# A two-layer gated cross-attention block: layer 0 also stores its turned context to DRAM, and layer 1 loads it in place of a turn by DMA

## The reference, cut to what matters

```python
def reference(x, ctx_1024, ...):          # x: 16 x 56 x 128, ctx_1024: 16 x 1500 x 128
    x = x + tanh(g_xattn[0]) * L0_xattn(ctx_1024, ctx_1024, layernorm(x), mask, ...)  # 16 heads of 8
    x = x + tanh(g_ffn[0])   * L0_ffn(layernorm(x), ...)       # top-1 of 8 experts + a shared one
    x = x + tanh(g_xattn[1]) * L1_xattn(layernorm(x), ctx_1024, ...)                  # 16 heads of 64
    x = x + tanh(g_ffn[1])   * L1_ffn(layernorm(x), ...)       # ternary weights, 8-bit activations
    return x
```

## Time and profile before

| | |
|---|---|
| median of 3 runs | 1309.55 us (1305.81 to 1319.06) |
| profiled execution | 1312.12 us, of which the span is 1310.4 us |
| TensorE (PE) busy | 1144.0 us, 87% |
| VectorE (DVE) busy | 892.8 us, 68% |
| ScalarE (ACT) busy | 698.3 us, 53% |
| GpSimd (POOL) busy | 510.6 us, 39% |
| DMA queue of SP | 147.11 MB, 54.8% of 16 engines |
| HBM | 61.93 MB read, 12.80 MB written |

### The profile page before, as it was taken

How to read it: one execution, slowest core, us unless ns; L and a number is a source line. 1 busy time by engine, 2 the same in 40 slices (tenths; PEclk the granted TensorE clock), 3 DMA queues, 4 the chain that set the end, 5 groups by cost and what they waited for, 6 DMA issues and landing times.

```text
span 1310.4 us, 27967 instructions
## 1 busy us (share of the span) xinstructions
PE 1144.0 (87%) x10056; PEld 654.3 (50%) x10056; DVE 892.8 (68%) x1250; ACT 698.3 (53%) x967; POOL 510.6 (39%) x344
## 2 busy tenths in 40 slices
PE   0769899999999998777879889899999989899974
PEld 0335556665665656533434455454555545455542
DVE  6456666666666673687777667677576857767668
ACT  0435455555555555445666546466465656556542
POOL 5157766666765633234022222323232322222220
PEclk9979899999999999699999999899999999999996
DMA  5144344443444353003029987989688888988530
GB/s 158 50 127 138 109 123 125 135 137 121 127 135 139 115 126 80 6 2 47 1 55 155 142 145 142 153 141 154 130 159 144 148 152 147 155 147 151 106 69 15
DMA packets 271256, 151.00 MB, mean 115 GB/s; under 512 B 233713, under 2 KB 244449, under 8 KB 271201
## 3 DMA queue, kind: packets, MB, share of 16 engines
q1 hardware_dynamic: 264944, 147.11, 54.8%
q10 hardware_dynamic: 6256, 3.16, 1.0%
HBM read 61.93 MB, written 12.80 MB: 57 GB/s over the span
## 4 chain that ended last, share of the span: by engine, by line
PE 62%; DVE 12%; issue 8%; ACT 6%; DMA 5%; SPq 3%; ACTq 3%; POOL 0%; DVEq 0%; POOLq 0%
PE bank L853 11%; PE bank L871 11%; PE bank L728 7%; PE bank L752 6%; PE bank L756 5%; PE bank L769 4%; PE bank L821 4%; DMA region<-wg_sb 3%; ACTq L385 3%; DVE neg_max L1546 2%; DMA region<-u_w 2%; DVE region L1696 2%; SPq L462 2%; DVE e_row L1507 2%; PE bank L829 2%
## 5 line engine op out<-in xcount | busy, mean ns | idle before, releaser
L1507 DVE CUSTOM_DVE_ANT_0 e_row<-bank,region 112x1500 f32<-112x1500 f32 x128 | 220.1, 1720 | 125.4 <-PE bank L728 124.0
L1201 ACT ACTIVATE region<-bank 125x896 f32<-125x896 f32 x192 | 176.0, 917 | 202.6 <-PE bank L756 202.6
L1546 DVE TENSOR_REDUCE neg_max<-bank 128x1 f32<-128x1500 f32 x112 | 192.5, 1719 | 126.5 <-PE bank L853 126.3
L853 PE MATMUL bank<-region 128*128 128x500 f16 x1008 | 234.5, 378 | 3.2 <-ACT e_row L1228 1.8
L1237 ACT COPY region<-bank 128x768 f16<-128x768 f16 x224 | 177.9, 794 | 108.0 <-PE bank L821 108.0
L1228 ACT ACTIVATE e_row<-bank,neg_shift 128x1500 f32<-128x1500 f32 x112 | 169.2, 1511 | 81.8 <-DVE neg_shift L1550 41.8
L554 POOL CAST u_w<-e_row 128x1500 f16<-128x1500 f32 x56 | 80.6, 1440 | 242.1 <-ACT e_row L1228 214.3
L554 POOL CAST wg_sb<-e_row 128x1500 f16<-128x1500 f32 x56 | 83.1, 1484 | 211.6 <-ACT e_row L1228 147.5
L853 PEld LDWEIGHTS bank<-region 128*128 (+1 forms) x1008 | 97.3, 98 | 108.3 <-issue 4.0
L752 PE MATMUL bank<-row_of,region 112*128 112x448 bf16 x384 | 137.7, 359 | 7.9 <-ACT region L1201 7.9
L871 PE MATMUL bank<-region 125*128 125x384 f16 (+1 forms) x576 | 130.8, 359 | 14.5 <-DMA region<-wg_sb 12.0
(11 more groups left out here) (218 smaller groups left out, 1524.4 us busy)
## 6 DMA issues: line engine op xcount, KB each, us to landing
region<-region SPq DMA_DIRECT2D x192, 96.0 KB, 2.2
region<-split_rows SPq DMA_DIRECT2D x72, 250.0 KB
c_in<-in_ctx SPq DMA_DIRECT2D x16, 750.0 KB
split_rows<-region SPq DMA_DIRECT2D x16, 750.0 KB
region<-in_mask_Bx1xSxS_if SPq DMA_DIRECT2D x32, 328.1 KB
g_w<-split_rows SPq DMA_DIRECT2D x24, 250.0 KB
x_norm_t<-inverse_rows SPq DMA_DIRECT2D x16, 256.0 KB, 4.6
x_norm_t<-inverse_rows SPq DMA_DIRECT2D x16, 192.0 KB, 6.6
```

The source lines that it names most:

```text
L853: last = pe.matmul(score_banks1(par, t)[:, k, :], q1[:, ql, b, 128 * t:128 * (t + 1)], c_t1[par][:, 4 * k:4 * k + 4, cl, 0:KP], start=(ql ...
L1201: act.activation(p0[:, 2 * i:2 * i + 2, :], ring0("s", h, i)[0:KP, :, 0:HALF_ROWS], ACT.Exp, scale=SCALE0)\
L1507: dve.tensor_tensor_reduce(out=masked.rearrange("p (a k) -> p a k", a=3), in0=bank[0:R0, 0:3, 0:4 * KP], in1=mask_bias[par][:].rearrange(" ...
L1546: dve.tensor_reduce(neg_max[:, t:t + 1], score_banks1(par, t), AX.XY, ALU.max, negate=True)\
```

## The change

Layer 0 gets one more transfer per batch: behind the stacking copies SP stores `c_t0` whole, 768 KB, to a DRAM tensor `turned_rows[b]` of the same layout. ScalarE waits for the store of the batch before ahead of its next copy into `c_t0`. Layer 1 no longer loads `split_rows` for a turn and no longer turns the context by DMA: at t = 1 and t = 3 of a batch SP loads the high and the low half of `turned_rows[b + 1]`, 384 KB each, straight into the next batch's `c_t1`, whose layout is now [feature, n, c, p] instead of [feature, c, n, p]. TensorE's scores wait for these loads where they waited for the turn. The buffer `c_split1` is left unused in its place. `split_rows` and the loads into `c_keep1` stay.

```diff
--- before.py
+++ after.py
@@ -221,11 +221,11 @@
         out1_w = carve([128, H, 128])
         assert queries_dead <= (B - 3) * ROWS // 2 and scores_dead <= hole_at
         assert at[0] == split_at
-        c_split1 = carve([128, KC, 2, E], F16)
+        carve([128, KC, 2, E], F16)
         c_keep1 = [carve([128, KC, 2, E], F16)[0:KP],
                    g_w[:].rearrange("p e i -> p (e i)")[0:KP, 0:KC * E].bitcast(F16)
                    .rearrange("p (c n e) -> p c n e", c=KC, n=2)]
-        c_t1 = [carve([128, KC, 2, 128], F16) for _ in range(2)]
+        c_t1 = [carve([128, 2, KC, 128], F16) for _ in range(2)]
         GROUPS1 = [(0, 4), (4, T1)]
         before_p1 = at[0]
         p1 = [carve([128, 2, KC, 128 * (b - a)], F16) for a, b in GROUPS1]
@@ -260,6 +260,7 @@
 
         inverse_row = place[0:4].rearrange("p g d -> p (g d)")
         split_rows = nc.dram_tensor("split_rows", [B, KP, KC, 2, E], F16, kind="Internal").ap()
+        turned_rows = nc.dram_tensor("turned_rows", [B, 128, 2, KC, 128], F16, kind="Internal").ap()
         inverse_rows = nc.dram_tensor("inverse_rows", [2, ROWS], F32, kind="Internal").ap()
 
         bank = ctx.enter_context(nc.psum_tensor("bank", [128, 8, 512], F32))
@@ -410,12 +411,16 @@
             wait_apart(sp, "sp", (sem("low0"), b + 1))
             sp.dma_start(split_rows[b], c_split0[0:KP].rearrange("p c n g d -> p c n (g d)")).then_inc(sem("split_out0"), 16)
 
-        def sync_split_in(sp, b, third):
-
-            if third == 0:
-                wait_apart(sp, "sp", (sem("c_turned1"), 16 * b))
-            part = slice(4 * third, 4 * third + 4)
-            sp.dma_start(c_split1[0:KP, part], split_rows[b, :, part]).then_inc(sem("split_in1"), 16)
+        def sync_turned_out(sp, b):
+
+            wait_apart(sp, "sp", (sem("ct_done0_1"), b + 1))
+            sp.dma_start(turned_rows[b], c_t0).then_inc(sem("turned_out0"), 16)
+
+        def sync_turned_in(sp, b, par, n):
+
+            if n == 0:
+                wait_apart(sp, "sp", (sem("scores1"), (b - 1) * T1))
+            sp.dma_start(c_t1[par][:, n], turned_rows[b, :, n]).then_inc(sem("turned_in1"), 16)
 
         def sync_keep(sp, b, par, third):
 
@@ -454,13 +459,6 @@
             sp.dma_start(x_norm_t[:, 128 * a:128 * z],
                          inverse_rows[par, 128 * a:128 * z].unsqueeze(0).broadcast_to((128, 128 * (z - a))))\
                 .then_inc(sem("inverse1"), 16)
-
-        def sync_turn_context1(sp, b, par):
-
-            wait_apart(sp, "sp", (sem("split_in1"), 48 * (b + 1)))
-            wait_apart(sp, "sp", (sem("scores1"), (b - 1) * T1))
-            sp.dma_start_transpose(c_t1[par].rearrange("p c n k -> p (c n) k"), c_split1.rearrange("p c n e -> p (c n e)"))\
-                .then_inc(sem("c_turned1"), 16)
 
         @block.sync
         def _(sp):
@@ -489,33 +487,30 @@
                     if not (isinstance(b, int) and b + 2 >= B):
                         sync_load_context(sp, b + 2, par)
                     sync_stack(sp, b + 1, 1 - par)
+                    sync_turned_out(sp, b + 1)
                     if not (isinstance(b, int) and b + 2 >= B):
                         sync_load_mask(sp, b + 2)
             sync_split_out(sp, 0)
             sync_stack(sp, 0, 0)
+            sync_turned_out(sp, 0)
             sync_load_mask(sp, 1)
             batches(sp, layer0)
 
             sp.wait_ge(sem("split_out0"), 16 * B)
-            sp.wait_ge(sem("ct_turned0"), 2 * B)
-            for third in range(3):
-                sync_split_in(sp, 0, third)
+            sp.wait_ge(sem("turned_out0"), 16 * B)
             sp.wait_ge(sem("st0"), B * 2 * NP)
             load(sp, "in_down0", [
                 (d_w[:, 0:NE].rearrange("p e c h -> p (e c) h"), rt_down.rearrange("e (c p) h -> p (e c) h", p=128)),
                 (d_w[:, NE], sh_down.rearrange("(c p) h -> p c h", p=128))])
 
-            sync_turn_context1(sp, 0, 0)
-            for third in range(3):
-                sync_split_in(sp, 1, third)
+            for n in range(2):
+                sync_turned_in(sp, 0, 0, n)
             sp.wait_ge(sem("w_tern"), 3)
             for third in range(2):
                 sync_keep(sp, 0, 0, third)
 
             def layer1(b, par, first, last):
                 sync_keep(sp, b, par, 2)
-                if not last:
-                    sync_turn_context1(sp, b + 1, 1 - par)
                 for t in range(T1):
                     sync_turn1(sp, b, par, t)
                     if t == 1 and not first:
@@ -526,8 +521,8 @@
                         sync_inverse_out1(sp, b, par, 0)
                     if t == 5:
                         sync_inverse_back1(sp, b, par, 0)
-                    if 1 <= t < 4 and not (isinstance(b, int) and b + 2 >= B):
-                        sync_split_in(sp, b + 2, t - 1)
+                    if t in (1, 3) and not last:
+                        sync_turned_in(sp, b + 1, 1 - par, t // 2)
                     if t >= 5 and not last:
                         sync_keep(sp, b + 1, 1 - par, t - 5)
             batches(sp, layer1)
@@ -846,12 +841,12 @@
 
         def pe_scores1(pe, b, par, t):
             if t == 0:
-                pe.wait_ge(sem("c_turned1"), 16 * (b + 1))
+                pe.wait_ge(sem("turned_in1"), 32 * (b + 1))
             wait(pe, sem("exp_done1"), b * T1 + t - 1)
             for k in range(3):
                 for ql, cl in ((0, 0), (0, 1), (1, 0)):
                     last = pe.matmul(score_banks1(par, t)[:, k, :], q1[:, ql, b, 128 * t:128 * (t + 1)],
-                                     c_t1[par][:, 4 * k:4 * k + 4, cl, 0:KP],
+                                     c_t1[par][:, cl, 4 * k:4 * k + 4, 0:KP],
                                      start=(ql == 0 and cl == 0), stop=(ql == 1))
             last.then_inc(sem("scores1"), 1)
 
@@ -1248,6 +1243,7 @@
 
             act.wait_ge(sem("ct_turned0"), 2 * b + n + 1)
             if not (isinstance(b, int) and b == 0):
+                act.wait_ge(sem("turned_out0"), 16 * b)
                 for g in range(G):
                     act.wait_ge(sem(f"stack{1 - par}_{g}"), per_use(b - 1, 1 - par, 48))
             act.copy(c_t0[:, n].rearrange("p c k -> p (c k)"),
```

## The result

The changed kernel takes 1270.44 us (median of 4 runs, 1268.9 to 1271.89) against 1308.74 us for the kernel before (4 runs, 1305.81 to 1319.06): a ratio of 0.9697, 95% interval 0.965 to 0.9744. Its profiled execution took 1269.61 us with a span of 1267.3.

The account below looks back on a forecast made before the run. TensorE was taken to bound both attentions, with only layer 1 leaving gain, in waits from SP's queue. Waits of 13.1 and 19.2 us plus 9.3 us of clock made 41.6 us off 1309.55: 1267.9, with 1 us left over 1269, range 1259 to 1296.

Parts of the forecast that it names:

- part 1: Layer 1: dropping turn L462 ends TensorE's waits at L845 (13.1 us), L871 (19.2 us) and clock losses (9.3 us): 41.6 us.
- The clock's 9.3 us: Layer 1, after 700 us: TensorE work lost to lowered clock after waits, five stretches, one of 2.5 and four of 1.7 us.
- rival C: Layer 1: second load late, L853 waits; 1 us late per batch 1284, 3 us late 1339; in full, with D, 0.07.
- The check by pairs: Layer 1: two batches of 72.94 us without L871 stall, less 1.82 idle and 1.7 clock, give 69.4 us per pair.
- The last even batch as a trial by itself: Layer 1: with turn L462 but no split_in, L845 still waits 2.13 us and L871 doesn't wait.
- part 2: Layer 1 loads: two narrow loads ahead of tile 3 cost 3.9 us at 129 GB/s, one wide 1.8 us at 215.
- part 3: Layer 1: second load behind tile 3's turn reaches the next batch's first score product with 1.2 to 2.4 us slack.
- part 4: Layer 0: the store flows 3.6 us, cost 0, or 24 us if the next context load's delay isn't taken up.
- A: Layer 1: the forecast case, all waits of both sorts go; 1262 to 1280 us, chance 0.60.
- D: Layer 0: delayed context load isn't taken up, 1293 us, or 1329 with a 6.0 us store; in full, with C, 0.07.
- E: Layer 1: nothing happens, TensorE's waits are VectorE's and ScalarE's; 1300 to 1310 us, 0.13 with mixes within 1%.
- B: Layer 1: only SP's issue time mattered, DMA engines stay full, L871's stalls remain; 1293 us, 0.20 with mild C or D.

Follow-up runs that it names:

- run 11: Changed kernel with both loads of the turned rows at the head of the batch instead of behind tiles 1 and 3: 1276.75 us, ratio 0.9731.
- run 2: Kernel before without layer 1's split-context loads at t = 1 to 3, turn by DMA kept: 1287.24 us, ratio 0.9813.
- run 3: Kernel before with the turn by DMA left out after the first two batches, loads kept: 1270.94 us, ratio 0.9676.
- run 12: Kernel before with the context's turn issued as two turns of six chunks at its old place, the batch's head: 1311.06 us, ratio 0.9999.
- runs 5: Kernel before with the turn in two halves behind tiles 1 and 3, its loads at t = 5, 6 and the next head; no store: 1309.46 us, ratio 1.0006.
- run 4: Kernel before with stored split rows padded from 125 to 128 partitions and the loads for the turn made with 128: 1288.72 us, ratio 0.9817.
- run 10: Kernel before with the turn in halves behind tiles 1 and 3, loads moved later, all split-row transfers on 128 partitions, no store: 1266.72 us, ratio 0.9656.
- run 6: Changed kernel with its second load issued behind tile 4's turn instead of tile 3's: 1317.53 us, ratio 1.0059.
- run 1: Kernel before plus only layer 0's store of the turned halves and ScalarE's wait on it: 1310.21 us, ratio 0.9983.
- run 7: Changed kernel storing the turned halves three times per batch, to three tensors, in layer 0: 1288.18 us, ratio 0.9844.
- Runs 9: Kernel before with the turn in halves behind tiles 1 and 3 and no split-context loads after batch 1: 1270.65 us, ratio 0.9686.
- run 8: Changed kernel with split rows padded to 128 partitions, for the split store and kept-context loads: 1268.08 us, ratio 0.9696.

## Why the prediction was right

**The sum (part 1).** Forecast 41.6 us, and 1269 us with one left over. Measured 38.3 us between the medians, 42.5 between the profiled executions, 41.2 in layer 1's stage. By its terms: L845's 13.1 us, gone; L871's 19.2 us, gone. The clock's 9.3 us can be held against TensorE's busy time for the same 3773 products of layer 1, before and after:

```profile
663.00:1277.00 614.00, 562.07 (x3773) 310.43 (x3774) 432.30 (x521) 359.59 (x493) 166.84 (x114) 0.98 0.80 138
662.00:1234.00 572.00, 553.18 (x3773) 306.48 (x3772) 427.42 (x514) 358.41 (x492) 165.59 (x114) 0.99 0.65 131
```

That is 8.9 us less, of 9.3 forecast, and the clock is 1.00 in each stretch from 700 to 1200 us. One premise was too general: a wait of 1.8 us doesn't always lower the clock. The kernel before waits 1.82 us at 1060.38 as at 987.44, but the clock is 1.00 from 1060 to 1066 and 0.66 from 987 to 992; and run 11, with waits of up to 1.9 us, has 1.00 over 700 to 1200. The sum counted only stretches whose fall it had seen, so it came out right; rival C's price of 1.7 us for each late load rests on the general form. The check by pairs gave 69.4 us for a pair without waits; measured 69.42. Nothing was late next: TensorE stands at 99.5 of 100 us.

**Two causes.** The last even batch as a trial by itself gave the right reading: run 2 lost L871's stalls and kept L845's wait (forecast 1284, measured 1287), run 3 lost nearly all of both (1270, 1271). The prediction said that the issue time of L462 makes the first wait, and for the kernel before that holds: tile 0's turn is issued late there (2.1 us at 824.07, and 2.8 us at 976.68, ahead of the wait of the earlier trace rows; 2.9 us in run 12) and lands in its usual 3.8 us. But it is one of two means. In runs 5 and 11 the turn is issued in time, within 0.3 us of the product that it waits for, and lands late, after 8.8 and 5.3 us. What both have in common is work in the queue ahead of tile 0's turn, and the change takes it away. One sign missed: tile 0's turn was to go out within 1 us of its low half, and goes out 3.4 us behind it (805.70, 809.12), since the prediction overlooked that it also waits for the product with V. In the sum this made no difference. With the turn landing at 812.9 and VectorE's next low half in that place at 813.15, the margin in the changed kernel is 0.2 us, which is why run 11's 1.5 us more of landing shows at once.

**The loads (part 2).** Narrow transfers at 129 GB/s against 215 was the right reading, and too small in its effect: run 4 won 24 us where I expected 14, run 10 against run 5 some 46 us by the ratios. In the changed kernel the store and the mask load behind it reach 0.98 of the engines and 300 GB/s, and the split store after them, with its 125 partitions, 0.32 and 132:

```profile
426.00:428.00 2.00, 2.00 (x39) 1.20 (x38) 1.67 (x2) 0.88 (x2) 1.92 (x2) 1.00 0.32 132
...
446.00:448.00 2.00, 2.00 (x40) 1.20 (x38) 1.85 (x2) 0.45 (x2) 0.64 (x1) 1.00 0.98 300
```

By the rule of the Trainium skill's "DMA: Bandwidth & Descriptors" ("Why a DMA increments its semaphore by 16 and not by 1") 125 partitions use 5 of 16 engines, 0.31, and 128 use all; the trace agrees. That a narrow load delays a turn on all 16 engines, by filling 5 of them, fits all these runs, but which engines are busy the profile's rows don't show.

**The second load's place (part 3).** Forecast slack 1.2 to 2.4 us; run 6 shows 3.1: the term was too careful, since the load lands in 3.6 us from its issue and isn't added whole to the turn ahead. That the place is a tight one is right: one tile later it costs some 47 us, with 31.7 us of waits; the granted clock of 0.97 to 0.98 over the stage's 570 us makes up about the rest.

**The store (part 4).** Cost 0 forecast, and none that run 1 could tell from 0. Landing 3.8 us against 3.6 us worked out for its flow. The limit lies between one and three stores, at the context load, as part 4 had named it, and not at ScalarE's copy, which never waited for a store.

**The rivals.** A came. C is run 6, one place away: with 2.2 us of lateness per batch it is slower than the kernel before, as the point worked out for it (some 2 us) said. D is run 7. E is refuted, since L845's wait went with the queue's work. B (the engines stay as full) is refuted by the share of 0.66 and by run 3, but its rule has a true side that I had weighed as against the trace. The page "Advanced Engine Details and Errata" ("X-Bar Transpose (TRN2)") of the Trainium skill says that turns are as fast as plain transfers. Runs 9 and 10 agree so far as that the turn by DMA need not cost anything here. What cost was where it stood and what stood with it.

## What to carry to other kernels

A queue shared by urgent and patient transfers is read by what stands ahead of the urgent one: spread patient transfers between urgent ones, and test the order before replacing the transfer (run 10 got the whole gain with the old one, at the price of wide rows). Padding a transfer of 125 partitions to 128 is worth a try where a queue is crowded (24 us in run 4); where nothing waits for the queue it gains nothing (run 8). When a gain rests on a transfer placed late in such a queue, measure its slack by placing it one step later, since one step here was the difference between 0.970 and 1.006.

## What I had not expected of the hardware

SP's issue of a 384 KB turn takes 1.4 us on a free queue and up to 5.3 us behind other transfers (run 5), and a turn of 768 KB 6.0 us whole or as two halves back to back (run 12). The issue time of a DMA in the profile thus depends on what stands ahead of it. And padding by three rows, which adds bytes, moved some 46 us (run 10 against run 5, by their ratios).
